# Four value projections computed from rounded weight parts instead of full fp32, and right operands built by 16 sums instead of 20

## The reference

```python
Q = (x @ Wq);  K = (ctx @ Wk);  V = (ctx @ Wv)            # per head, width 512
score = einsum('bhqd,bhkd->bhqk', Q, K) / sqrt(512)
attn  = softmax(where(mask != 0, score, -inf))
out   = einsum('bhqk,bhkd->bqhd', attn, V) @ Wo + x
result = (out - mean) * rsqrt(var + 1e-5) * gamma + beta
```

## Time and profile before

| | |
|---|---|
| median of 3 runs | 354.6 us (354.4 to 354.69) |
| profiled execution | 354.68 us, of which the trace's span is 352.9 us |
| PE busy | 347.1 us (98%) |
| DVE / ACT / POOL busy | 285.6 / 238.8 / 201.1 us |
| first stage on PE, from its first projection to the first product of the second stage | 4.40 to 123.94 us |
| granted TensorE clock, mean | 0.996 of full speed |

### The profile page before, as it was taken

The page is one execution under the profiler, slowest core; times in us unless marked ns, Lnnn a source line. Parts: engine busy times, 40 slices in busy tenths (PEclk is TensorE's granted clock), DMA queues, the critical chain, the costliest instruction groups (busy, mean ns, idle before and its releaser), DMA issues.

```text
span 352.9 us, 6849 instructions
## 1 busy us (share of the span) xinstructions
PE 347.1 (98%) x2272; PEld 323.5 (92%) x2272; DVE 285.6 (81%) x523; ACT 238.8 (68%) x790; POOL 201.1 (57%) x212
## 2 busy tenths in 40 slices
PE   9999999999999999999999999999999999999994
PEld 6999999999999999998899899889988998899884
DVE  2159999999866467898798888987987989889896
ACT  3267766545555669887886976977778769768560
POOL 0045654400004858689769688688696796884243
PEclk9999999999999999999999999999999999999998
DMA  7999758775645070053142341440532423413012
GB/s 235 425 418 321 275 227 336 286 255 211 220 158 190 0 285 15 4 178 120 61 172 68 119 151 55 156 150 33 179 105 75 158 72 131 149 46 105 32 50 101
DMA packets 19683, 55.81 MB, mean 158 GB/s; under 512 B 1728, under 2 KB 3264, under 8 KB 17728
## 3 DMA queue, kind: packets, MB, share of 16 engines
q1 hardware_dynamic: 18784, 54.38, 42.2%
q10 hardware_dynamic: 864, 1.00, 1.1%
HBM read 46.98 MB, written 8.39 MB: 157 GB/s over the span
## 4 chain that ended last, share of the span: by engine, by line
PE 98%; DVE 0%; DVEq 0%; issue 0%
PE pair L670 30%; PE pair L595 27%; PE pair L480 17%; PE pair L487 15%; PE pair L657 5%; PE pair L585 1%; PE pair L692 1%; PE pair L687 1%; DVE centred L1187 0%; DVEq L103 0%; DVE stats_last L1179 0%; DVE mean_var L1184 0%; DVE var_eps L1159 0%; PE pair L605 0%; DVE out_sb L1173 0%
## 5 line engine op out<-in xcount | busy, mean ns | idle before, releaser
L670 PE MATMUL pair<-vw_hi,pt_hi 128*128 128x512 f32 x155 | 62.3, 402 | 0.0
L670 PE MATMUL pair<-vw_hi,pt_lo 128*128 128x512 f32 x155 | 60.9, 393 | 0.0
L670 PE MATMUL pair<-vw_lo,pt_hi 128*128 128x512 f32 x155 | 60.6, 391 | 0.0
L1312 POOL TENSOR_TENSOR out_sb<-centred,beta_sb 128x512 f32<-128x512 f32 x30 | 38.8, 1294 | 29.2 <-ACT centred L864 29.1
L1363 POOL TENSOR_TENSOR w_proj_lo<-w_proj,w_proj_hi 128x768 fp32r<-128x768 f32 x14 | 25.7, 1859 | 39.1 <-ACT w_proj_hi L755 39.1
L819 ACT ACTIVATE prob<-c,neg_max 128x77 f32<-128x77 f32 x128 | 43.9, 346 | 0.0
L480 PE MATMUL pair<-kv_t,w_out_hi 128*128 128x308 f32 x160 | 42.0, 336 | 0.0
L1357 POOL TENSOR_TENSOR xo_lo<-x_sum,xo_hi 128x512 fp32r<-128x512 f32 x32 | 41.4, 1299 | 0.5 <-ACT xo_hi L843 0.5
L595 PE MATMUL pair<-a_hi,xo_hi 128*128 128x308 f32 x128 | 40.4, 316 | 0.0
L1332 POOL TENSOR_TENSOR x_sum<-xt_in 128x256 f32<-128x256 f32 x16 | 11.9, 745 | 47.6 <-DMA xt_in<-x_tiles 47.4
L595 PE MATMUL pair<-a_hi,xo_lo 128*128 128x308 f32 x128 | 38.9, 304 | 0.0
(11 more groups left out here) (121 smaller groups left out, 1021.1 us busy)
## 6 DMA issues: line engine op xcount, KB each, us to landing
w_out<-wo SPq DMA_DIRECT2D x8, 1024.0 KB, 4.8
xt_in<-x_tiles SPq DMA_DIRECT2D x16, 512.0 KB, 4.0
x_in<-x_rows SPq DMA_DIRECT2D x16, 512.0 KB, 4.8
out<-out_sb SPq DMA_DIRECT2D x31, 256.0 KB, 2.2
w_out<-wq_t SPq DMA_DIRECT2D x7, 1024.0 KB, 7.6
w_proj<-wv SPq DMA_DIRECT2D x8, 768.0 KB, 4.7
w_proj<-wk SPq DMA_DIRECT2D x6, 768.0 KB, 9.6
w_out<-wq_t SPq DMA_DIRECT2D x2, 512.0 KB, 8.1
```

The costliest lines, as they stand in the source:

```text
L670: mm = pe.matmul(ps_out[:, i % 2, 0:s.model], ps[:, j, :], v[:, b, j, :], start=(j == 0 and n == 0), stop=(j == s.key_t - 1 and n == len(p ...
L1312: pool.tensor_tensor(out_sb[i % OUT_RING][:, :], centred[i % 2][:, :], beta_sb[:, :], ALU.add)\
```

## The change

Uses 12 to 15 (value projections 4 to 7) become short: `whole` is now true for uses 0 to 2 and 10, 11 alone. So ACT rounds and POOL splits `w_proj` for four more uses, and DVE takes two operations a half for P(12), P(13), P(14) in place of one and adds `add_kv` for P(15). The wait for `dve_vw_lo` before m = 2 now stands in `project` as well.

For this the buffers move. `w_proj_hi` lies in the last two blocks of `vw_hi` and `vw_lo`, which are written late; `vw_hi` and `vw_lo` are therefore laid out block first, batch second. `ctx_split` moves behind `vw_t`. The temporaries of T get their own places (`t_tmp4`, `t_tmp5`), the latter where `xt_in` lies. The zeroing of the unfilled rows of `vw_hi` and `vw_lo` (four memsets of 32x512 at the program's start) becomes two of 32x1024 in use 14, after P(15).

The right operands need 8 sums a batch, not 10, in the order T1, T2, T3, T4. T1, T2 and T3 are formed in use 8 and split in use 9; T4 is formed in use 10, rounded by ACT in use 11, and split by DVE in use 12.

```diff
-    FROM_FULL = H + 2
+    FULL_VALUES = (H + 2, H + 3)
-    T_STEPS = {T1: 3, T2: 5, T4: 7, T3: 10}
+    T_ORDER = (T1, T2, T3, T4)
+    T_STEPS = {T1: 3, T2: 5, T3: 6, T4: 8}
...
         def whole(u):
-            return u < FULL_PROJ or u >= FROM_FULL
+            return u < FULL_PROJ or u in FULL_VALUES
...
             def project(u):
...
-                        pe.wait_ge(act_p_hi, 2 * (u - FULL_PROJ) + half + 1)
-                        pe.wait_ge(pool_p_lo, 2 * (u - FULL_PROJ) + half + 1)
+                        pe.wait_ge(act_p_hi, 2 * rounded_before(u) + half + 1)
+                        pe.wait_ge(pool_p_lo, 2 * rounded_before(u) + half + 1)
                         wait_kv(u - 1, half)
+                    if m == 2 and u > H + 1:
+                        pe.wait_ge(dve_vw_lo, sum(len(part) for part in plan[:u - 1 - H]))
...
@@ scalar, loop over u
+                if u == H + 3:
+                    for part in T_PARTS[6:]:
+                        round_t(*part)
                 take_out_product(u, 1)
@@ vector
-            for v in (vw_hi, vw_lo):
-                for b in range(s.batches):
-                    dve.memset(v[PAD_FROM:P, b, s.key_t - 1, :].bitcast(F32), 0.0).then_inc(dve_pad, 1)
+            def clear_pads():
+
+                dve.wait_ge(pe_proj, 2 * USES)
+                for v in (vw_hi, vw_lo):
+                    dve.memset(v[PAD_FROM:P, s.key_t - 1, :, :].bitcast(F32), 0.0).then_inc(dve_pad, 1)
...
                 if u == H:
                     right_sum(T1, 0)
+                elif u == H + 4:
+                    split_t(T4, 0)
+                    split_t(T4, 1)
...
+                if u == USES - 2:
+                    clear_pads()
                 if not whole_out(u):
                     add_out_product(u, 0)
...
+                elif u == H + 2:
+                    for b in range(s.batches):
+                        right_sum(T4, b)
@@ gpsimd
-            for u in range(FULL_PROJ, FROM_FULL):
+            for u in (v for v in range(USES) if not whole(v)):
```

More of the change, by code:

```diff
@@ L94, in build @@
     KT = s.model_t // 2
-    T_STEPS = {T1: 3, T2: 5, T4: 7, T3: 10}
-    T_PARTS = [(n, b) for n in (T1, T2, T4, T3) for b in range(s.batches)]
+    T_ORDER = (T1, T2, T3, T4)
+    T_STEPS = {T1: 3, T2: 5, T3: 6, T4: 8}
+    T_PARTS = [(n, b) for n in T_ORDER for b in range(s.batches)]
     t_no = {part: n + 1 for n, part in enumerate(T_PARTS)}
@@ L157, in build @@
         with ExitStack() as spare:
-            t_tmp4 = [spare.enter_context(nc.sbuf_tensor(f"t_tmp4_{b}", [P, KT, s.half], F32)) for b in range(s.batches)]
+            t_tmp4 = [spare.enter_context(nc.sbuf_tensor(f"t_tmp4_{n}", [P, KT, s.half], F32)) for n in range(3)]
         w_out_hi1 = sb("w_out_hi1", [P, s.model_t, s.dim_t, P], F32R)
@@ L161, in build, with vw_and_proj @@
         a_lo = sb("a_lo", [P, s.model_t, s.batches, s.row], F32R)
-        vw_hi = sb("vw_hi", [P, s.batches, s.key_t, s.model], F32R)
-        vw_lo = sb("vw_lo", [P, s.batches, s.key_t, s.model], F32R)
+        w_proj_hi = []
+        def vw_and_proj(name, n):
+            with ExitStack() as early:
+                early.enter_context(nc.sbuf_tensor(f"vw_first{n}", [P, FREE_VW, s.batches, s.model], F32R))
+                w_proj_hi.append(early.enter_context(nc.sbuf_tensor(f"w_proj_hi{n}", [P, s.dim_t, s.ctx_t, P], F32R)))
+            return sb(name, [P, s.key_t, s.batches, s.model], F32R)
+        vw_hi = vw_and_proj("vw_hi", 0)
+        vw_lo = vw_and_proj("vw_lo", 1)
+        with ExitStack() as spare:
+            t_tmp5 = [spare.enter_context(nc.sbuf_tensor(f"t_tmp5_{n}", [P, KT, s.half], F32)) for n in range(3)]
         xt_in = [sb(f"xt_in{n}", [P, CHUNK, s.model]) for n in range(XT_RING)]
-        with ExitStack() as early:
-            w_proj_hi = [early.enter_context(nc.sbuf_tensor(f"w_proj_hi{n}", [P, s.dim_t, s.ctx_t, P], F32R))
-                         for n in range(2)]
         t_hi0 = sb("t_hi0", [P, 3, KT, s.half], F32R)
@@ L320, in summed_kv, with rounded_before @@
             return whole_out(u) and not whole(u)
+        def rounded_before(u):
+            return sum(not whole(v) for v in range(u))
         def split_before(u):
@@ L686, in last_out_rows @@
                         for n, (ps, v) in enumerate(passes):
-                            mm = pe.matmul(last_ab[:, half, :], ps[:, j, :], v[:, b, j, cols], start=False,
+                            mm = pe.matmul(last_ab[:, half, :], ps[:, j, :], v[:, j, b, cols], start=False,
                                            stop=(j == s.key_t - 1 and n == len(passes) - 1), skip_group_check=True)
@@ L976, in split_kv @@
             def split_kv(u):
+                if u > H and not whole(u):
+                    dve.wait_ge(dve_t_lo, t_no[T2, 1])
                 for half in range(2):
@@ L1047, in right_sum @@
                     dve.wait_ge(dve_a_lo, 2 * H)
[L1048 to L1051, removed]
+                elif n == T4:
+                    dve.wait_ge(act_t_hi, t_no[T1, b])
+                    dve.wait_ge(dve_t_lo, t_no[T1, b])
                 done = t_done(n, b) - len(steps_of(n))
```

73 lines of the change are left out of this document (29 added, 44 removed).

## The result

The changed kernel takes 356.42 us (median of 6 runs, 356.08 to 356.87), the kernel before 354.68 us beside it (6 runs, 354.4 to 355.15). The ratio is 1.0048, with a 95% interval from 1.0035 to 1.0061: slower by 1.7 us. Predicted were 355.8 us, 1.2 us above the 354.6 that the prediction started from.

A forecast was written before the change was run, and what follows sets the result against it. PE was taken to bound the kernel, holding 98% of the chain. 354.68 - 0.48 (short projections) + 1.6 (wait in P(14)) + 0.1 (wait at O(15)) = 355.9 us profiled, 355.8 as median; range 354.0 to 357.0.

The forecast's parts named there:

- The saving: On PE, four projections made short: each takes 3.03 us instead of 3.15, saving 0.12 us a projection, 0.48 us for four.
- the projections run at their column count: Rival: short projections on PE take 2.36 us, 0.79 saved each, 3.2 in all; 351.4 to 353.1 us; chance 1%.
- P(12) and P(13) are covered: The added ACT, POOL and DVE work for P(12) and P(13) makes PE wait nothing, with 0.5 us to spare at P(13).
- The order of turns in use 12: T4's DVE splits alternate with POOL's split for P(14), `vw_lo` ends at 106.1, and PE loses 1.6 us in P(14).
- The rival in which DVE asks first: Use 12: T4's splits don't collide with POOL's, `vw_lo` ends at 104.4, before PE wants it; 354.2 us; chance 22%.
- P(14)'s rest, and what lies behind: P(14)'s rest on DVE ends at 110.6, before PE's transposes in O(13) at 110.75; cost nothing, with 0.15 us of cover.
- The wait at O(15): Two new memsets of 0.9 us each delay `vw_t` of O(14) to 119.8; PE wants it at 119.7: 0.1 us, between 0 and 0.2.
- The sum: Whole kernel: 354.68 - 0.48 + 1.6 + 0.1 = 355.9 us profiled, 355.8 as median; own range 355.2 to 356.5; chance 58%.
- the one in P(14): PE's wait for `vw_lo` in the middle of P(14): 1.6 us in all, bounds 0 and 2.1.
- The clock: Rival: the wait lowers TensorE's clock for some 3 us and PE loses half of that; 357.4 us; chance 3%.

## Why the prediction was right, and where not

**The saving.** 0.12 us a projection, 0.48 in all: right, 0.11 and 0.45 by the marks. That the projections run at their column count, 0.79 saved each, is refuted.

**P(12) and P(13) are covered.** Right. POOL splits for P(13) from 92.20 (predicted 92.39), and PE waits for neither.

**The order of turns in use 12.** Right to 0.2 us, step by step:

| step | predicted | measured |
|---|---|---|
| POOL's split for P(14) starts | 99.62 | 99.45 |
| T4's first split asks | 100.00 | 99.77 |
| T4's first split ends | 102.12 | 101.96 |
| POOL's half 1 ends | 103.83 | 103.69 |
| T4's second split ends | 104.49 | 104.35 |
| `vw_lo` ends | 106.1 | 105.93 |
| PE wants it | 104.6 | 104.43 |
| lost, by the marks | 1.6 | 1.72 |

The prediction said that the second split would be recorded at 2.3 us; its own times give 2.44, and 2.46 was measured.

The rival in which DVE asks first needed 0.38 us, and the trace has a margin of 0.32. It comes from lags between the same engines, and all six executions of the kernel after lie above 356.

**P(14)'s rest, and what lies behind.** Right. The rest was predicted for 110.6, and its last operation ends at 110.39 (109.91 + 0.48), ahead of the transposes at 110.70. POOL's split for P(15) starts at 109.11 (109.15), and its sums end at 117.63 (117.5). SP issues the x tiles 0.5 us later than before, and POOL finds them there. None of this cost anything.

**The wait at O(15).** Here the size failed, by 0.7 us. The step was "the memsets are 0.9 each and DVE is free at 117.5, so `vw_t` ends at 119.8 and PE wants it at 119.7": 0.1 us. DVE was free at 117.47, a memset's row reads 0.91, and PE would have wanted it at 119.66. All three were right. What the sum left out are two things. The gaps ahead of the memsets, 0.27 and 0.16 us with some hundredths behind, are some 0.45 together. The time that PE takes to resume (0.16, and 0.07 behind it) I had counted for the first wait and not for this one.

The trace of before could have given the first of the two. There the small memsets at the program's start lie 0.545 us apart from start to start, not the 0.485 of the earlier trace rows:

```profile
0.90 1.03 DVE L951 MEMSET vw_hi<- 32x512 f32 x2 [0.90 <-PEq L1434]
1.99 1.02 DVE L951 MEMSET vw_lo<- 32x512 f32 x2
```

Two of them, as many elements as one new memset, take 1.09 us (0.90 to 1.99), and the new ones lie 1.08 apart. The bounds, 0 and 0.2, were the real error: the memset's own bounds, 0.5 and 0.97, bounded a recorded duration, while the term was the difference of two ends, to which every gap between them belongs.

**The sum.** With 0.81 in place of 0.1 the same sum gives 354.68 - 0.48 + 1.6 + 0.81 = 356.6 for the profiled execution, which took 356.40 us. The difference of 0.2 is about that by which its P(10) began earlier than that of the kernel before. The range that the prediction gave the forecast itself, 355.2 to 356.5, holds the median of 356.42, but its lower end follows from none of the bounds: with 0 for both waits the sum is 354.1. And the median lies near the upper end because the wait at O(15) came out four times its bound, while the one in P(14) stayed 0.4 below its own. That the total fell inside this narrow range is in part luck.

**The clock.** The forecast had it at 3%, since a wait of 1.6 us was shorter than 2 us of rest at the end of the program, in which it stayed at 1.00. That comparison didn't carry: after a wait of 1.5 us the clock fell in one profiled execution, and stayed up in another. Over the twelve executions of these two kernels the mean clock is below 0.996 in this one alone. It did not decide this result, but could have added some 1.6 us to it.

## What to carry to other kernels

Where an engine's operation from SBUF is moved, look at what the other engine does from SBUF at that moment: here a place 1.8 us earlier, or 1.6 us later for the second split, made the same instruction 0.79 us long instead of 2.2 to 2.5. The waits that the turns made cost 1.7 us, and the whole saving was 0.45. A term that comes out as the difference of two times (a margin of 0.1 us) needs the gaps between instructions and the time to resume in it, not the durations alone; starts of like instructions in a row show what one takes. And a piece of work that isn't wanted until the next stage, like the zeroing here, cost PE nothing in use 15, and 0.8 us ahead of `vw_t`, which PE was waiting for.

## What the runs showed of the hardware

- The clock can fall after a wait of 1.5 us in the middle of a full PE: in one profiled execution it did, in one of another kernel with the same wait it did not. After 2.9 us it did in the one that has windows, and by their mean clocks in the three others. It falls after PE has resumed, stays at half for some 3.4 us (0.50 in the windows between), and costs some 1.6 us where the marks can be read.
- Turns have an exception where two requests come almost together. In the kernel after, POOL's first split for P(12) and DVE's last two splits of T in use 9:

```profile
84.10 4.35 POOL L1373 TENSOR_TENSOR w_proj_lo<-w_proj,w_proj_hi 128x768 fp32r<-128x768 f32 x2 [17.91 <-ACT w_proj_hi L766]
```

```profile
83.45 1.50 DVE L1075 TENSOR_TENSOR a_lo<-t_tmp,a_hi 128x616 fp32r<-128x616 f32 x2
```

  DVE's pair is whole (1.50 us), though its second operation was issued at 84.16, 0.06 us after POOL's start. POOL ended 0.68 us later than 3.67 us would give, so it waited for both. Starts that lie within 0.1 us of each other don't tell who asked first.
- A memset of 32x1024 reads 0.91 us, about double the 0.485 of 32x512, and has 0.27 us ahead of the first and 0.16 between two in both places where it was tried. Two lie 1.08 us apart from start to start. Whether DVE idles in the gap or the row reads short, the runs don't show.
- A memset does not take turns with POOL's operations from SBUF, as DVE's subtractions of two SBUF operands do: one of POOL that was issued 0.41 us into a memset took its usual 0.73.
